# Count tables of two graph layers built in groups of 31 edge tiles with one column per node

## What is computed

```python
x = _layernorm(x + _L0_gnn_ref(x, edge_index, ...))   # mean of x[src] per dst, two 128x128 products
x = _layernorm(x + _L1_gnn_ref(x, edge_index, edge_attr_128, ...))   # an MLP for each edge, mean per dst
x = _layernorm(x + _L2_gnn_ref(x, edge_index, edge_attr_128, ...))   # sum of x_comb[src] per dst, MLP
x = _layernorm(x + _L3_gnn_ref(x, edge_index, ...))   # attention over the edges, softmax per dst

# layer 0
agg = jax.ops.segment_sum(x[src], dst, num_segments=n)
deg = jax.ops.segment_sum(jnp.ones((src.shape[0],), dtype=x.dtype), dst, num_segments=n)
mean_neigh = agg / jnp.maximum(deg, 1.0)[:, None]
return x @ w_self.T + b_self + mean_neigh @ w_neigh.T + b_neigh

# layer 2, the part that matters here
neigh = jax.ops.segment_sum(x_comb[src], dst, num_segments=num_nodes)
h = x_comb + neigh
```

## Time and profile before

| | us |
|---|---|
| median of 3 runs (6180.21 to 6195.2) | 6191.66 |
| the profiled execution, whole time | 6181.86 |
| its span, first to last instruction | 6180.0 |
| layer 0, first to last product of L662 | 50.7 to 847.5 |
| layer 2, first to last product of L1197 | 3270.1 to 3806.3 |

### The profile page before, as it was taken

How to read it: one execution, slowest core, us unless ns; L and a number is a source line. 1 busy time by engine, 2 the same in 40 slices (tenths; PEclk the granted TensorE clock), 3 DMA queues, 4 the chain that set the end, 5 groups by cost and what they waited for, 6 DMA issues and landing times.

```text
span 6180.0 us, 70833 instructions
## 1 busy us (share of the span) xinstructions
PE 4521.5 (73%) x24017; PEld 3636.4 (59%) x24017; DVE 2509.1 (41%) x8563; ACT 1745.2 (28%) x3903; POOL 3125.5 (51%) x3324
## 2 busy tenths in 40 slices
PE   6999978889899899998998997234443444434445
PEld 5888865666666666666668996234343443434434
DVE  8999952333333333333335443123222222222324
ACT  5888841222222222222224553001110111101111
POOL 0000026666666666666650002666666666666664
PEclk9999989999999999999999998566666656666666
DMA  6777765555555555555546885222222222222221
GB/s 153 163 164 166 165 161 180 181 180 182 184 179 182 177 183 178 180 184 177 182 152 196 243 243 156 47 48 50 49 48 50 48 49 50 50 48 49 50 49 34
DMA packets 472464, 804.79 MB, mean 130 GB/s; under 512 B 72608, under 2 KB 301131, under 8 KB 462123
## 3 DMA queue, kind: packets, MB, share of 16 engines
q0 software_dynamic: 140192, 443.73, 28.9%
q1 hardware_dynamic: 317802, 346.76, 17.7%
q10 hardware_dynamic: 14112, 9.74, 0.5%
HBM read 663.72 MB, written 136.22 MB: 129 GB/s over the span
## 4 chain that ended last, share of the span: by engine, by line
PE 54%; another core or an unknown queue 24%; issue 9%; DVE 9%; DMA 2%; ACT 1%; POOL 0%; DVEq 0%; ACTq 0%; SPq 0%
PE bank L1028 17%; PE bank L1015 12%; PE bank L1197 7%; PE bank L682 5%; PE bank L662 2%; DVE ring L1335 2%; DMA atab<-at 2%; PE bank L1548 2%; PE bank L583 1%; DVE hs L631 1%; PE bank L964 1%; DVE hs L629 1%; DVE tops L1285 1%; PE bank L1528 0%
## 5 line engine op out<-in xcount | busy, mean ns | idle before, releaser
L543 POOL DMA_INDIRECT ring<-ptab,src x1612 | 1526.6, 947 | 829.4 <-issue 446.2
L543 POOL DMA_INDIRECT ring<-htab,src x1612 | 1539.4, 955 | 772.4 <-issue 465.4
L1028 PE MATMUL bank<-ring,oh 128*126 128x384 f32 x3224 | 1280.0, 509 | 80.8 <-issue 76.9
L981 DVE TENSOR_TENSOR ring<-bank,ring 128x512 f32<-128x512 f32 x806 | 540.3, 687 | 1588.6 <-remote 715.7
L1548 PE MATMUL bank<-ring,oh 128*126 128x132 f32 x3224 | 689.0, 348 | 552.4 <-issue 546.4
L1015 PE MATMUL bank<-w1e,ea 128*128 128x256 f32 x3224 | 896.8, 397 | 117.4 <-issue 89.0
L1548 PEld LDWEIGHTS bank<-ring,oh 128*126 128x126 f32 x3224 | 593.8, 249 | 622.4 <-issue 611.2
L1015 PEld LDWEIGHTS bank<-w1e,ea 128*128 128x128 f32 x3224 | 627.6, 198 | 393.1 <-issue 167.7
L1028 PEld LDWEIGHTS bank<-ring,oh 128*126 128x126 f32 x3224 | 624.4, 197 | 361.5 <-issue 155.6
L997 ACT ACTIVATE ring<-ring 128x1024 f32<-128x1024 f32 x403 | 425.4, 1056 | 1224.4 <-DVE ring L981 875.1
L682 PE MATMUL bank<-xhl,at 128*126 128x258 f32 x3822 | 712.4, 323 | 0.0
(11 more groups left out here) (271 smaller groups left out, 4466.9 us busy)
## 6 DMA issues: line engine op xcount, KB each, us to landing
atab<-at POOLq DMA_DIRECT2D x78, 1543.5 KB, 9.9
ring<-ea_r SPq DMA_DIRECT2D x403, 256.0 KB
ea<-ea_t SPq DMA_DIRECT2D x403, 256.0 KB
adjb<-atab SPq DMA_DIRECT2D x156, 535.5 KB, 4.7
adjb<-atab SPq DMA_DIRECT2D x78, 472.5 KB, 4.4
ring<-ptab,src POOLq DMA_INDIRECT x1612
ring<-htab,src POOLq DMA_INDIRECT x1612
ptab<-pO ACTq DMA_DIRECT2D x49, 128.0 KB, 7.3
```

Of the source, the lines that this page charges most:

```text
L543: return e.indirect_dma_start(o, None, table, bass.IndirectOffsetOnAxis(ap=src[:, t:t + 1], axis=0))
L981: e.tensor_tensor(group1(gi, m % 2), MLP[m % NM][:, :].rearrange("p (g f) -> p g f", g=2), group1(gi, m % 2), ALU.add).then_inc(s_edge, 1)
L1028: w = e.matmul(SUM[s % 2][0:SL, 0:384], slots_of(s, i), rv1[:, t // G % NR1, t % G, :], start=i == 0, stop=t == END[s])
```

## The change

Layers 0 and 2 get groups of their own, `GD` = 31 tiles each, 1612 = 52 x 31. A column of the group's table is now a node, counted from the group's first node, not a slot of a tile. A tile then writes five columns (`W5`) at an offset that the data decide, and the writes of neighbouring tiles overlap: a node at the end of a tile is left out of the tile's own five columns and gets code 5 instead, and its count is added into the next tile's bank by a second product (49 columns, with the one-hots of the tile before), whose column 0 is that node. The table has 128 columns for each source block, 52 tables of 6272 columns in place of 78 of 6174.

ScalarE reads the 31 offsets of a group into registers (`offsets`, L702) and places each tile's counts in two halves, source blocks 0 to 24 and 25 to 48. Each half waits until the same half of the tile before has been written, since the later one must win. Before each ACTIVATE stands a register instruction (`ISA` in the order below, named FUSED_REGOPS in a trace) that works out its address, two or three register operations; the waits stand on it. In layer 2 the parts of a table are 17, 17 and 15 blocks of 128 columns, and are asked for 16 positions ahead, not 11. A group may now touch three node blocks (17 of the 52 do), which takes a second VectorE instruction for its node matrix.

The preparation gets some twenty small VectorE instructions, three of them over 1611 or 1612 columns, a DMA of three rows, and a memset of `at0` on GpSimd; the other buffer's memset comes at the start of layer 0.

```diff
+W5 = S - 1
+GD = 31
...
+    DSTART, DSIZE, DB0, DB1 = groups(NT, FIRST, LAST, GD, 3)
+    DN = len(DSTART)
...
+            e.tensor_tensor(tmp[:, 0:NT - 1], d_cur[:, 0:NT - 1], d_head[:, 1:NT], ALU.is_equal).then_inc(s_prep_v, 1)
...
+            e.scalar_tensor_tensor(out=code0[:, 0:NT - 1], in0=tmp[:, 0:NT - 1], scalar=float(W5), in1=slot[:, 0:NT - 1],
+                                   op0=ALU.mult, op1=ALU.max).then_inc(s_prep_v, 1)
...
             def dense_hots(e, d, q):
...
                     if q >= NU:
-                        e.wait_ge(d.adj, q - NU + 1)
+                        e.wait_ge(d.adj, q - NU + 2)
...
-            def dense_counts(e, d, q):
+            def offsets(e, s):
+
+                return nc.values_load_multi_w_load_instructions(
+                    off0[0:1, DSTART[s]:DSTART[s] + GD], engines=[e.engine], min_val=0, max_val=P - W5,
+                    skip_runtime_bounds_check_because="the flag that chose this path bounds each offset in its group")[1]
+
+            def dense_counts(e, d, q, at):
                 if 1 <= q <= NT:
                     t = q - 1
-                    s, i, _ = where(t)
+                    s, i = dense_where(t)
+                    if i == 0:
+                        at[:] = offsets(e, s)
                     e.wait_ge(d.adj, t + 1)
...
-                    e.activation(AT[s % 2][:, :, S * i:S * i + S],
-                                 ADJ[t % 3][:, 0:S * NB].rearrange("p (b j) -> p b j", j=S), ACT.Copy).then_inc(d.count, 1)
+                    for k, h in enumerate((slice(0, HALF), slice(HALF, NB))):
+                        if t:
+                            e.wait_ge(d.count, 2 * t - 1 + k)
+                        e.activation(AT[s % 2][:, h, bass.ds(at[i], W5)],
+                                     ADJ[t % 3][:, 0:W5 * NB].rearrange("p (j b) -> p b j", b=NB)[:, h, :],
+                                     ACT.Copy).then_inc(d.count, 1)
...
             def dense_adjacency(e, d, q):
                 if q < NT:
                     e.wait_ge(d.hot, 2 * q + 2)
                     if q >= 3:
-                        e.wait_ge(d.count, q - 2)
-                    e.matmul(ADJ[q % 3][:, 0:S * NB], hotU[:, q % NU, :], hotV[:, q % NU, 0:S * NB], start=True,
-                             stop=True).then_inc(d.adj, 1)
+                        e.wait_ge(d.count, 2 * (q - 2))
+                    m = e.matmul(ADJ[q % 3][:, 0:W5 * NB], hotU[:, q % NU, :], hotV[:, q % NU, 0:W5 * NB], start=True,
+                                 stop=q == 0)
+                    if q:
+                        m = e.matmul(ADJ[q % 3][:, 0:NB], hotU[:, (q - 1) % NU, :], hotV[:, (q - 1) % NU, W5 * NB:S * NB],
+                                     start=False, stop=True)
+                    m.then_inc(d.adj, 1)
...
-                    for h in range(NB * i // n, NB * (i + 1) // n):
+                    for h in range(NB * i // GD, NB * (i + 1) // GD):
...
+            LEAD2 = 16
...
-                u, c = 3 * g + h // THIRD, h % THIRD
-                        m = e.matmul(SUM[g % 2][0:SL, 0:256], adj[:, u % 3, c * SL:c * SL + SL], yhl[:, h, :],
+                        m = e.matmul(SUM[g % 2][:, 0:256], adj[:, u % 3, c * P:c * P + P], yhl[:, h, :],
```

More of the change, by code:

```diff
@@ L45, in plan, with groups @@
     return nb, nt, lo, hi, first, last
-def groups(nt, first, last):
+def groups(nt, first, last, tiles=GT, blocks=2):
     start, t = [], 0
@@ L52, in groups @@
         start.append(t)
-        t = next((u for u in range(t + 1, min(t + GT, nt)) if last[u] - first[start[-1]] > 1), min(t + GT, nt))
+        t = next((u for u in range(t + 1, min(t + tiles, nt)) if last[u] - first[start[-1]] >= blocks),
+                 min(t + tiles, nt))
     size = [b - a for a, b in zip(start, start[1:] + [nt])]
@@ L119, in build @@
     SPLIT = 4097.0
-    PIECE = next(n for n in range(2048, 0, -1) if NB * SL % n == 0)
+    PIECE = next(n for n in range(2048, 0, -1) if NB * P % n == 0)
     assert max(LAST[t] - FIRST[t] for t in range(NT)) <= 1 and max(B1[s] - B0[s] for s in range(NS)) <= 1
@@ L128, in build @@
         LASTS.setdefault(SHI[b], []).append(b)
+    assert all(n == GD for n in DSIZE)
+    DEND = [a + n - 1 for a, n in zip(DSTART, DSIZE)]
+    DLO = [min(s for s in range(DN) if DB0[s] <= b <= DB1[s]) for b in range(NB)]
+    DHI = [max(s for s in range(DN) if DB0[s] <= b <= DB1[s]) for b in range(NB)]
+    DLASTS = {}
+    for b in range(NB):
+        DLASTS.setdefault(DHI[b], []).append(b)
     ctx = ExitStack()
@@ L199, in build @@
         small = sb("small", [P, 64])
+        dnode = small[:, 8:8 + DN]
         flag = sb("flag", [P, 8])
@@ L321, in prep_pool @@
             e.memset(brow[:, :], 0.0).then_inc(s_clear, 1)
+            e.memset(at0[:, 0, :].bitcast(F32), 0.0).then_inc(s_clear, 1)
         def prep_sync(e):
@@ L768, in pool0 @@
             def pool0(e):
-                for s in range(NS):
-                    e.wait_ge(d0.count, END[s] + 1)
+                e.memset(at0[:, 1, :].bitcast(F32), 0.0).then_inc(d0.clear, 1)
+                for s in range(DN):
+                    e.wait_ge(d0.count, 2 * (DEND[s] + 1))
                     e.dma_start(atab[s * P:(s + 1) * P, :].rearrange("p (k c) -> p k c", c=PIECE),
@@ L811, in tensor0 @@
                     dense_sums(e, d0, q)
-                    for b in LASTS.get(ADDS0.get(q), []):
-                        add_nodes(e, b, 129, 128, d0.node, d0.kept, 1, s_mean0, 6, d0.add)
+                    for b in DLASTS.get(ADDS0.get(q), []):
+                        add_nodes(e, b, 129, 128, d0.node, d0.kept, s_mean0, 6, d0.add)
                     for b, k in W0.get(q, []):
@@ L1868, in lay_out @@
     ends[3, :nt] = [P * (c - b + 1) for b, c in zip(first, last)]
-    out["dends"] = np.ascontiguousarray(ends.reshape(4, -1, P).transpose(2, 0, 1))
+    dstart, dsize, db0, _ = groups(nt, first, last, GD, 3)
+    ends[4, :nt - 1], ends[4, nt - 1] = head[1:], head[-1]
+    ends[5, :nt - 1] = 1
+    ends[6, nt - 1] = 1
+    ends[7, :nt] = np.repeat(head[dstart], dsize)
+    out["dends"] = np.ascontiguousarray(ends.reshape(8, -1, P).transpose(2, 0, 1))
+    out["dgroups"] = np.stack([head[dstart], np.array([P * b for b in db0], np.int32),
+                               head[np.array(dstart) + np.array(dsize) - 1]]).astype(np.int32)
     out["dslots"] = np.ascontiguousarray(np.repeat(slots, S, axis=1).T)
```

213 lines of the change are left out of this document (130 added, 83 removed).

## The result

The changed kernel takes **6712.02 us** (median of 4 runs, 6708.32 to 6716.02), the kernel before 6191.84 on the same chip (4 runs, 6180.21 to 6195.2): a ratio of **1.084** (95% interval 1.0825 to 1.0863). The forecast of 6140 us and its range of 6040 to 6240 are both missed, and the sign is wrong.

What follows compares the result with a forecast made beforehand. TensorE was taken to bound layer 2, VectorE and TensorE to be near their limit in layer 0, with ScalarE binding there after the change. Terms -148 + 7 + 91 + 2 = -48 us, from 6187 to 6140 us, range 6040 to 6240.

Steps and rivals of the forecast that it cites:

- the ScalarE part: Layer 0: ScalarE's halves at 530 ns a tile, register loads 24 us, other ACTIVATEs 10 us; 888 us, +91 us.
- the chain: Layer 0, ScalarE: wait, register instruction, hand-over and ACTIVATE from one half to the same half next tile; 530 ns, 854 us.
- rival C: Layer 0: ScalarE's chain is longer, 0.60 us a tile, +204 us, whole about 6252 us; chance 0.24.
- rival E: Layer 0: TensorE's clock falls from more gaps; 6168 us at 0.83, 6300 or more near half the clock; chance 0.04.
- the prediction's own test: Layer 0, ScalarE: forecast wrong if the register instruction takes under 60 ns or a register address slows the ACTIVATE.
- rival B: Layer 0: register work hidden or cheap, ScalarE under 0.49 us a tile, VectorE binds; about 6035 us; chance 0.26.
- Layer 2: TensorE's products and node additions there become fewer, copies stay hidden; -148 us, 388 us from first to last product.
- Rival D: Layer 2 misses its gain as fetches and copies don't keep up; 450 us instead of 388, whole 6200; chance 0.04.
- Preparation: Before layer 0: new VectorE instructions delay the input split and the weights' bias chain; +7 us.
- the two tails: Stretches after layers 0 and 2: +2 us after layer 0's last tile; layer 2's 3 us counted within its -148.

Runs made afterwards that it cites:

- e2: The changed kernel with each group's 31 offsets starting every 32 words, so all loads begin on a 16-byte step; 5754.64 us, ratio 1.033.
- e3: e2 with the whole row of offsets one word later, so no load begins on a 16-byte step; 6202.09 us (one run), ratio 1.114.
- e8: e2 with a 32nd, unused word in each load; 6264.46 us (one run), ratio 1.012.
- e1: The changed kernel with eight registers loaded once and reused, nearly all address instructions gone, counts in wrong columns; 5415.0 us, ratio 0.973.
- e5: e2 with the wait for the tile before moved from the address instruction to the ACTIVATE; 6336.31 us (one run), ratio 1.024.
- e7: e5 and e6 together: wait on the ACTIVATE, offsets in four loads of eight aligned words a group; 6146.94 us, ratio 0.994.
- e6: The changed kernel with a group's offsets loaded in four loads of eight aligned words, waits unmoved; 6269.14 us, ratio 1.013.
- after: The changed kernel itself, against the kernel before; 6712.02 us, ratio 1.084.
- e4: The changed kernel with four offsets packed in each word, 8 registers a group, taken apart by shift and mask; 5650.27 us, ratio 1.015.

## Why the prediction was wrong, step by step

**The step that failed** is a clause of the ScalarE part: "one register took 463 ns, and the chain stands still meanwhile: 52 x 0.46 = 24 us, *if 31 cost what one does*". They don't. The term measured **515 us**, and e2, e3 and e8 show that it goes by words and by their place. The row that it was taken from shows one register; the prediction bounded the term from one side only, while the parts of the chain beside it got two. The upper bound was in reach: 31 x 0.463 = 14.4 us a group, 746 us in all, and the truth lies between. The remark in rival C that 31 registers "may take longer than one" had no price.

The Trainium skill would have corrected it, had I read past the page that I cited. Its DMA: Bandwidth & Descriptors (Latency and other measured facts) gives a floor of about 600 ns for a tensor_load; here one word takes 0.463 us and 8 aligned ones 0.547, both somewhat under it. Its page Runtime: NRT & Kernel Launch (Instruction fetch mechanics) says that such a load, there one from HBM, costs about 200 ns a register even in bulk. By that the term would be 52 x 31 x 0.2 = 322 us, an estimate, and the sign would have come out right. The trace agrees for e3's first load, 6.6 us for 31 words off the step with no store under way (these come from SBUF); the later ones cost 0.39 a word and 32 aligned ones 0.06.

**A second loss came behind the first.** Layer 0 without the loads was forecast at 864 us and measures 942. The median distance would make it less: 1612 x 0.478 = 771, under the 778 (483 ns a tile) at which the other engines bind in e1. So 942 - 778 = 164 us are neither loads nor the median chain. The trace's records divide them. Of the 1560 distances inside groups 556 lie where the granted clock was at its lower level, and they average 690 ns: 556 x (0.690 - 0.483) = 115 us. The other 1004, at the full clock, average 535 ns: 1004 x (0.535 - 0.483) = 52 us, together 167. The first part is the clock behind the stalls. The second is the chain with the early wait: e2, where it stands early too, averages 535 ns at the full clock, and e5, where only the wait was moved, 492. That is **rival E** in part: its clock fell (to 0.75, not 0.83), but as a result of the stalls, not of many small gaps, and without stalls it stays at 0.98 (e1).

**The chain** was built rightly and sized too high: 530 ns forecast, 478 measured at the median. The ACTIVATE has its 270 ns (285 measured), the address instruction 46 in place of 130 to 189, and the hand-overs between them 478 - 285 - 46 = 147 where I had 70 to 167. One tile at 608 us shows them in the forecast's order: the first half's ACTIVATE lasts 298 ns, the wait instruction starts 30 ns after its end, the address instruction 55 ns after that start, and the next tile's ACTIVATE 93 ns later, 476 together. In an undisturbed stretch of ScalarE after the load (timeline, start us, length us), twelve halves run like this:

```profile
607.19 2.80 ACT L721 ACTIVATE at<-bank 128x125 f32 x12
```

(2.80 - 0.28) / 11 x 2 = 0.46 us a tile. That layer 0 averages 535 ns a tile at the full clock, close to the 530 forecast, is luck: the forecast had no waits of ScalarE for TensorE in it (136.5 us between 100 and 1400 us) and an address instruction three times too long.

By the prediction's own test, a register instruction under 60 ns, the forecast is wrong and **rival B**'s premise (under 0.49) true; by its test of the distance (under 0.45 is B, 0.53 the forecast) 478 lies between. B's sum is almost e1's result: 152 us less forecast, 153 measured, though e1 has hardly an address instruction. By this the chain alone should cost next to nothing; beside stalls it costs 120 us of layer 0, as e7 against e6 shows, since at 478 ns there is no room to make up for a stall.

The rule of Perfetto Trace Analysis in the Trainium skill (Per-engine timelines), by which a sequencer-only instruction waits in the sequencer and an ACTIVATE in a wait queue, agrees: a tenth of e5's distances is below 330 ns, and after has hardly one under 455.

**Rival C** gave the right sign and a wrong cause. Its 0.60 us came true only in e4, and then its layer 0 was 7 us off.

**Layer 2** was right: 388 us forecast and 384.8 measured, products 0.118 us apart. The groups of the page show the copies hidden and TensorE's one wait as short as in the earlier trace rows:

```profile
L1284 PE MATMUL bank<-yhl,adj 128*128 128x256 f32 x2548 | 355.9, 293 | 11.9 <-DVE yhl L1173 11.9
```

**Rival D** is out. **Preparation** was +10 us, not +7, and the two tails +15 together, not +2; they weren't looked into.

**The sum by its terms**: -151 + 10 + 15 + 660 = +534. Layer 0 was forecast at +91, 24 for the loads and 67 for the rest; it measured 515 and 145 (942 - 797). So 491 of the 569 us by which layer 0 was missed are the load term, and 78 the rest, which is the size of the clock's share above the 535 ns of the full clock, 556 x (0.690 - 0.535) = 86 us.

## What to carry to other kernels

Loading registers from memory took time by the word here, while the engine's own instructions stood still: count the words, put them on a 16-byte step in whole fours, keep each load shorter than the lead of the engines that wait (here three banks; at 0.36 to 0.48 us a tile an estimate of 1.1 to 1.4 us, whose edge no run measured), and keep it out of the time of a large transfer. When a computed address is needed, let the address instruction run ahead and put the wait on the instruction that uses it. And when a price comes from a row with one item, and the change has 31, write down both "as one" and "31 times one" before the sign of the forecast is settled.

## What the runs showed of the hardware that I had not expected

- A TENSOR_LOAD of 31 words off a 16-byte step takes 12.0 us (6.6 in e3's first, with no DMA moving); on a step 3.3 us (2.4 for the first); 32 words on a step 1.97; 24 words 1.50; 16 words 1.02; 8 words 0.547, little more than the one word of the earlier trace rows, 0.463.
- 8 aligned words take 1.7 us while a table's store of 1568 KB keeps the DMA engines busy.
- An address instruction takes 46 ns on ScalarE's sequencer, a shift or mask 38; but from start to start they take 63 to 66, so that the shift and mask of a tile, put behind the wait, lengthened the chain by 121.
- With the wait on the address instruction hardly a tile follows the last in under 455 ns (median 478); with the same wait on the ACTIVATE a tenth do in under 330 (medians in halves 362 to 472, as far as the other engines hold it up).
- Where TensorE had stood still for 12 us, the next 3.6 us were granted 0.50 of its clock, 1.2 GHz, with TensorE busy in 3.58 of them, and the 4 us after those 0.85.
